# Four-corner sum of a deformable sampling layer: two VectorE additions replaced by accumulating identity products on TensorE

## What is computed

```python
offset = conv2d(x, p_w, p_b, 1, 1); m = sigmoid(conv2d(x, m_w, m_b, 1, 1))
...                                    # p: a position for each pixel and each of 9 taps
x_off = g_lt * gather(qx_lt, qy_lt) + g_rb * gather(qx_rb, qy_rb) \
      + g_lb * gather(qx_lt, qy_rb) + g_rt * gather(qx_rb, qy_lt)
x_off = x_off * m
return conv2d(x_off, conv_w, None, stride=KS, padding=0)
```

## Time and profile before

| | us |
|---|---|
| executions: lowest, median, highest | 5537.7, 5557.2, 5562.9 |
| span of the profiled execution, first to last instruction | 5506.2 |
| first gather starts, last gather starts | 1664.9, 5441.8 |
| POOL, DVE, PE, ACT busy in the whole span | 2996.6, 1916.6, 2229.8, 1088.6 |

### The profile page before, as it was taken

How to read it: one execution, slowest core, us unless ns; L and a number is a source line. 1 busy time by engine, 2 the same in 40 slices (tenths; PEclk the granted TensorE clock), 3 DMA queues, 4 the chain that set the end, 5 groups by cost and what they waited for, 6 DMA issues and landing times. The chain is left out here.

```text
span 5506.2 us, 66353 instructions
## 1 busy us (share of the span) xinstructions
PE 2229.8 (40%) x22290; PEld 1582.0 (29%) x22290; DVE 1916.6 (35%) x3805; ACT 1088.6 (20%) x2072; POOL 2996.6 (54%) x3032
## 2 busy tenths in 40 slices
PE   5888888399972221212221211222221221222223
PEld 4777776277751111111111110111111111111112
DVE  4555555666652232222312322221222232222232
ACT  2545555277760000000000000000000000000002
POOL 4333333700006666666676666667576666666764
PEclk9888888699975555555555555555555555555555
DMA  5555555300041111111111111111111111111111
GB/s 168 159 158 167 166 160 164 99 7 0 0 154 43 43 43 44 47 46 43 44 48 45 42 46 45 42 45 48 40 48 46 43 45 45 47 45 41 48 43 65
DMA packets 182621, 368.15 MB, mean 67 GB/s; under 512 B 56040, under 2 KB 80360, under 8 KB 182072
## 3 DMA queue, kind: packets, MB, share of 16 engines
q1 hardware_dynamic: 99512, 195.54, 12.3%
q0 software_dynamic: 82944, 170.04, 11.2%
HBM read 252.10 MB, written 103.23 MB: 65 GB/s over the span
## 5 line engine op out<-in xcount | busy, mean ns | idle before, releaser
L1148 POOL DMA_INDIRECT l_got<-sample_table,l_tidx x2592 | 2528.2, 975 | 1350.0 <-issue 870.9
L1217 ACT ACTIVATE l_sampt<-l_samp 96x384 f32<-96x384 f32 x288 | 140.3, 487 | 3392.4 <-remote 1773.8
L1392 PE MATMUL l_out<-l_sampt,l_wout 96*32 96x128 f32 x1152 | 280.5, 414 | 1222.2 <-issue 1017.0
L1306 DVE TENSOR_TENSOR l_got<-l_got,l_weight 128x1152 f32<-128x1152 f32 x288 | 390.7, 1357 | 1071.0 <-DMA l_got<-sample_table,l_tidx 631.4
L1387 PE MATMUL l_samp<-l_ident,l_samp 128*96 128x128 f32 x864 | 245.5, 420 | 1126.1 <-DVE l_samp L1310 671.0
L1392 PEld LDWEIGHTS l_out<-l_sampt,l_wout 96*32 96x32 f32 x1152 | 167.4, 162 | 1328.6 <-issue 1050.4
L1387 PEld LDWEIGHTS l_samp<-l_ident,l_samp 128*96 128x96 f32 x864 | 124.7, 180 | 1244.7 <-DVE l_samp L1310 708.3
L473 DVE TENSOR_REDUCE l_mx<-l_s 128x2 f32<-128x392 f32 x590 | 304.0, 557 | 318.1 <-PE l_s L597 306.6
L931 PE MATMUL l_g<-l_hid,l_whh 128*128 128x192 f32 x1536 | 406.6, 347 | 0.0
L1392 PE MATMUL l_tab<-l_sampt,l_wout 96*32 96x128 f32 x576 | 142.8, 420 | 596.0 <-issue 518.5
L391 ACT ACTIVATE l_pt<-l_st 98x1024 f32<-98x1024 f32 x288 | 293.4, 1023 | 330.2 <-PE l_st L612 329.8
(11 more groups left out here) (157 smaller groups left out, 3987.5 us busy)
## 6 DMA issues: line engine op xcount, KB each, us to landing
l_kst<-k_parts SPq DMA_DIRECT2D x51, 882.0 KB, 6.4
l_got<-sample_table,l_tidx POOLq DMA_INDIRECT x2592
l_qst<-q_parts SPq DMA_DIRECT2D x51, 576.0 KB, 8.3
k_parts<-l_kp SPq DMA_DIRECT2D x26, 882.0 KB, 4.6
sample_table<-l_tab SPq DMA_DIRECT2D x52, 392.0 KB
k_parts<-l_kp SPq DMA_DIRECT2D x26, 588.0 KB, 4.0
q_parts<-l_qp SPq DMA_DIRECT2D x26, 576.0 KB, 4.7
q_parts<-l_qp SPq DMA_DIRECT2D x26, 384.0 KB, 3.8
```

The source lines that it names most:

```text
L1148: pool.indirect_dma_start(out=got[:, b, n, :], out_offset=None, in_=table, in_offset=bass.IndirectOffsetOnAxis(ap=at, axis=0)).then_inc(ga ...
L1306: dve.tensor_tensor(corners, corners, w, ALU.mult).then_inc(weighted, 1)
L1392: mm = pe.matmul(out_ps[c][C * b:C * (b + 1), 0:P], wout[:, q, :], sampt[:, b % 2, q, :], start=(q == 0), stop=(q == 2))
```

## The change

The two additions on VectorE go. The multiplication no longer writes in place but into a new buffer `prods`, two slots of 128 x 4 corners x 9 taps x 32 channels, corner first. TensorE now makes, for each third of the taps, four accumulating products: `prods` of one corner is the stationary operand, the identity the moving one, so that the sum over the corners appears turned in PSUM, where the three transposes had left it. The semaphores `reduced` and `summed` go; `weighted`, raised by the multiplication, now both lets POOL refill a slot and lets TensorE begin. VectorE waits in each unit for `samp_turned` of two units earlier; the semaphore starts at 2, and ScalarE's threshold is raised by 2.

```diff
-        red = sb("red", [P, 2, NTAP, 2 * C])
-        samp = sb("samp", [P, 2, NTAP, C])
+        prods = sb("prods", [P, 2, 4, NTAP, C])
...
                     for b in range(B):
-                        wait_apart(pool, reduced, t * B + b + 1, pool_passed)
+                        wait_apart(pool, weighted, t * B + b + 1, pool_passed)
...
-                        act.wait_ge(samp_turned, u + 1)
+                        act.wait_ge(samp_turned, u + 3)
                         act.wait_ge(convolved, u + 1)
...
-            dve.sem_inc(reduced, RING)
+            dve.sem_inc(weighted, RING)
...
                 dve.wait_ge(gathered[b], 16 * NTAP * (t + 1))
-                corners = got[:, b, :, :].rearrange("p n (k c) -> p (n k) c", c=C)
-                w = weight[:, bass.ds(t, 1), b, :, :].rearrange("p o n k -> p (o n k)").unsqueeze(2).to_broadcast([P, NTAP * 4, C])
-                dve.tensor_tensor(corners, corners, w, ALU.mult).then_inc(weighted, 1)
-                dve.wait_ge(weighted, u + 1)
-                dve.tensor_tensor(red[:, b % 2], got[:, b, :, 0:2 * C], got[:, b, :, 2 * C:4 * C], ALU.add).then_inc(reduced, 1)
-                dve.wait_ge(reduced, u + 1 + RING)
-                dve.tensor_tensor(samp[:, b % 2], red[:, b % 2, :, 0:C], red[:, b % 2, :, C:2 * C], ALU.add).then_inc(summed, 1)
+                w = weight[:, bass.ds(t, 1), b, :, :].rearrange("p o n k -> p (o n) k").unsqueeze(3).to_broadcast([P, NTAP, 4, C])
+                dve.wait_ge(samp_turned, u + 1)
+                dve.tensor_tensor(prods[:, b % 2].rearrange("p k n c -> p n k c"), got[:, b].rearrange("p n (k c) -> p n k c", c=C),
+                                  w, ALU.mult).then_inc(weighted, 1)
...
-                        if b >= 2:
-                            dve.wait_ge(samp_turned, t * B + b - 1)
                         unit(t, c, b)
...
             pe.sem_inc(convolved, 2)
+            pe.sem_inc(samp_turned, 2)
...
-                        pe.wait_ge(summed, u + 1)
+                        pe.wait_ge(weighted, u + 1 + RING)
                         for q in range(3):
-                            mm = pe.transpose(samp_ps[b % 2][0:3 * C, P * q:P * (q + 1)],
-                                              samp[:, b % 2, 3 * q:3 * q + 3, :].rearrange("p n c -> p (n c)"), ident[:, :])
+                            for k in range(4):
+                                mm = pe.matmul(samp_ps[b % 2][0:3 * C, P * q:P * (q + 1)],
+                                               prods[:, b % 2, k, 3 * q:3 * q + 3, :].rearrange("p n c -> p (n c)"), ident[:, :],
+                                               start=(k == 0), stop=(k == 3))
                         mm.then_inc(samp_turned, 1)
```

More of the change, by code:

```diff
@@ L1069, in deformable_layer @@
         weighted = sem("weighted")
-        reduced = sem("reduced")
-        summed = sem("summed")
         x_added = sem("x_added")
```

## The result

The changed kernel took 5754.4 us (median of four runs, 5741.3 to 5777.5), the kernel before 5560.0 (5537.7 to 5562.9) in the runs beside it: ratio **1.037, 95% interval 1.034 to 1.039**. It is slower, as forecast, but by 194 us and not by 1100: the forecast of 6660 and its range from 5950 both miss it.

What follows compares the result with a forecast made beforehand. The prediction took POOL's gathers plus its pauses for late TensorE results as the bound: 5557 us + 1144 for more pauses - 40 for less lengthened gathers = 6661, say 6660 us, range 5950 to 7450.

Steps and rivals of the forecast that it cites:

- TensorE's work is done late while POOL gathers: Gathers' stage: TensorE's results reach ScalarE some 23 us late, so POOL pauses 37 times, 479.2 us in all.
- The pace: TensorE in the gathers' stage: 127 records a tile instead of 43 give 1.88 pauses a tile, formerly one in two tiles.
- The pause: POOL's stop until TensorE's lateness is over and one unit is through: 12 us each, bounds 8.05 and 15.84 us.
- The second rival: TensorE is late per hand-over, not per record: late units get only 4.5 us longer, 6003 us; chance 0.07.
- The first rival: TensorE is prompt after all with denser units, POOL alone is the bound, its waits go: 5038 us; chance 0.09.
- VectorE's removed additions: 350 us of VectorE busy time goes; gathers lengthened less beside VectorE give back 0 to 78 us, taken as 40.
- The Trainium skill: Cited rule: two-SBUF-input VectorE operations hold up only GpSimd work reading SBUF; the 40 us would rest on descriptor writing counting.
- The 51 us: Whole kernel: the median, on which the sum was set, lies 51 us above the profiled execution's span of 5506.2 us.
- The new layout: VectorE's multiplication into another buffer, output in runs of 32: 1.357 us as now; even doubled, +1.4 us a unit is hidden.
- the moved waits: VectorE's wait for `samp_turned` also in units one and two, POOL's for the multiplication: cost nothing.
- The doubt about short pauses: After POOL pauses of about 5 us TensorE is late again; if 12 us also failed to clear it, 14600 us; chance 0.04.
- the fourth rival: Short POOL pauses don't clear TensorE's lateness, every record costs some 1.4 us: 178 us a tile, 14600 us; chance 0.04.

Runs made afterwards that it cites:

- B: Kernel before and changed kernel, both unchanged, run once more on a third chip: 5014.5 and 5016.5 us, ratio 1.0004.

## Why the prediction was wrong

**The sign was right, the size wrong, and the sign only for where it was taken.** Step by step:

- *"TensorE's work is done late while POOL gathers"*, the cause of the 479 us of waits. Right for the traces it was read from: 109 of the 288 copies come over 1 us late in the kernel before, and after the change the same signs stand there (26.1 us for 24 products). Wrong as a property of the kernel: the kernel before takes 5011 to 5020 us on five other chips, and neither its trace and those of its variants there nor the two of the changed kernel show it, with gathers at the same pace. What is different on the first chip (or at that time) no run here shows; I never met it again, so that the added records bring the loss there stayed untested. The first comparison alone speaks for it: 72 pauses instead of 37, in a kernel whose other parts were shown to be free elsewhere.
- *The pace*: "48 to 49 records pass promptly in the first 20 us, and then one in 2.8 us". This is the step that failed. It was fitted to one cycle of sparse units: nine records and then 22 us of nothing, so a time a unit was read as a time a record. With 24 records a unit the trace has 84 prompt records in 11.5 us, and late ones at 1.0 us in the same cycle. The sum's N, the pauses a tile, is 1.0 where I had 1.88. What sets the lateness in its place no run shows; the spread from 9.4 to 35.2 us for units of 30 records speaks against any fixed time a record.
- *The pause*: 9.9 us in the mean, where I had 12. With N = 1 and 9.9 the forecast's own sum gives 45.8 + 9.9 = 55.7 us a tile and 4010 us for the stage, +232 us; measured are +233.9 of waits. On the forecast's median, 5557 + 232 - 40 = 5749: the two numbers made the whole error of 900 us.
- *The second rival* (late per hand-over, 0.07, 6003 us) was nearer than the forecast. I had put against it that a hand-over's price needed another count to let records pass first. The evidence for it, "the 21 records begun at 3577.13 and the nine of a unit [...] were both seen 22 to 25 us late", has a third member in the cycle shown: 30 records from copy to copy in 30.3 us, where nine took 25.2. I had the first two in hand and gave them too little. But a fixed time a hand-over isn't shown either (9.4 to 35.2 us for 30 records), and the rival kept 36 pauses where 72 came: that it came nearer is in part luck.
- *The first rival* (TensorE prompt, 0.09, 5038 us) describes the other chips, but for both kernels, so there it is no gain: 5016.5 and 5014.5 (B).
- *VectorE's removed additions*, -40 us from gathers less lengthened. On the first chip the gathers got 23.9 us longer, on the third 6.8 shorter (65.0 against 71.8). The step took the lengthening for a price of VectorE's being busy. It comes from the phase between the multiply and the next gather, and the multiply stays. What lies beside the second addition is 0.04 us a gather, 10 us in all.
- *The Trainium skill* (SBUF — State Buffer, SBUF: two separate sides) calls the shared port pair an exclusive lock that a VectorE operation with two SBUF inputs holds against GpSimd work that reads SBUF. The gathers agree for one direction: they are blocked until the multiply ends, to 3 ns. It lets whichever begins first block the other; that isn't seen here for the multiply, which takes its 1.36 us also when it begins in the course of a gather.
- *The 51 us* around the span: 2 us in all other runs. The sum was set on the median, so the forecast does not rest on it.
- *The new layout* and *the moved waits* at nothing: right. The first two units of a tile never start late for the wait that is new in them; the 18 pauses inside a tile come from the third and fourth, which had it before. The multiply takes 1.356 us, and on the third and fourth chips the whole change comes out even (1.0004 and 1.0007).
- *The doubt about short pauses*: no pause train came; the fourth rival is out.

## What to carry to other kernels

If a profile shows an engine's results late by tens of microseconds for which its own queue has no reason, run the same kernel again elsewhere before building a sum on the lateness: here it was 544 of 5560 us, more than anything the change did, and absent on five chips. A rate read from sparse work (one unit, then idle) must not be carried to dense work. And where a software-issued gather bounds a stage, the moment at which a long two-input VectorE operation starts against the next gather is worth more than the operations removed beside it: begun 0.22 us later, it cost 0.22 us in the mean in 265 of 288 units.

## What the hardware showed that was not expected

- The same kernel took 5560 us on the first chip and 5011 to 5020 on five others, with a granted clock of 0.53 in the gathers' stage in both (and B), so the clock isn't the cause. The traces of the first chip also hold fewer recorded semaphore updates by DMAs (16053 against 51024 on the third, kernel before), and many waits there end in "remote" or "issue" in place of a named instruction. The loss lies where the lateness does: up to 1660 us both traces hold the same 9296, and behind that 6757 and 41728. That both come from one cause is a guess, and whether the recording of the trace takes part in the lateness was not tested.
- A gather that begins on GpSimd while VectorE's two-input multiply runs is longer by what the multiply still has to run, less 0.13 us. One that has begun is left alone.
- Small copies on VectorE overlap: four of 0.18 us in 0.42 us, and the multiply behind them begins before the last has ended.
- Eight times the transposes cost nothing where TensorE is prompt (four comparisons, 0.9989 to 0.9997), and in the changed kernel neither does TensorE's busy time, which on the third chip doubles from 857 to 1722 us between 1665 and 4960 us while its granted clock goes from 0.53 to 0.72 of full speed (B).
